# Signalling TensorE's finished groups with a drain in the two edge phases of a four-layer graph network

## The chip, the core and the metric

The kernel runs on one core of one Trainium2 chip. The metric is device time in microseconds (us), the median of several executions. A profile is one further execution, recorded by the hardware profiler. Its span runs from the first to the last recorded instruction.

## What is computed

The reference passes 12,500 node rows of 64 floats through four graph layers, with 200,000 edges sorted by destination. After each layer there is a residual sum and a layer norm. The change lies in the edge work of the last two layers, called Edge 2 and Edge 3 (layers are counted from 0):

```
# layer 2
se = concat([h[src], eh], -1)
msg = leaky_relu(se @ W_msg); q = concat([qrh, qeh], -1) @ W_q / temp; k = se @ W_k
att = sum(q * k, -1); alpha = softmax of att over the edges of one destination
agg = segment_sum(alpha * msg, dst)
# layer 3
combined = concat([node_features[src], edge_features], -1)      # 64 + 32 columns
h_l = relu(combined @ msg_w1[l] + msg_b1[l])                    # two inner layers l
agg = segment_sum(sum over l of (h_l @ msg_w2[l] + msg_b2[l]), dst) / (degree + 1e-8)
```

## The kernel before

The edges lie on 128 partitions, 1,568 on each. An edge phase takes them in chunks of J = 28 edges per partition. That makes 56 chunks, two to each pass of a loop, with buffers b = 0 and 1. Inside a chunk TensorE works in quads of 4 edges per partition, so 7 quads to a chunk, 392 in a phase. Every engine has an instruction stream of its own, written out by hand, and the streams meet only at semaphores. The sequencer of an engine takes its instructions in the order written.

**GpSimd (POOL)** gathers the source rows of a chunk with 28 indirect DMAs (L771). Before them it waits for the chunk's indices and for `rows_free[b]`, which says that the chunk two earlier in this buffer has been read.

**SyncE (SP)** goes chunk by chunk (`EdgePhase.sync`). It waits until the rows are gathered, loads the indices of the chunk two further on (L705), waits for `attr_free[b]`, loads that chunk's attributes (L709), waits for `ready[b]` and stores the finished sums (L712).

**TensorE (PE)** has two functions in each phase. `turn` transposes a quad of gathered and loaded rows into PSUM and then raises `turned`. `multiply` makes the products of a quad that was turned earlier and raises `multiplied`. The order in a chunk is turn 0, turn 1, multiply 0, turn 2, multiply 1, and so on. The last turn of a chunk comes after the sixth multiply instead of before it. After the last turn a drain raises `rows_free[b]`, and in Edge 2 a second drain raises `attr_free[b]`.

**ScalarE (ACT)** copies what was turned from PSUM to SBUF (`move`: L1383 and L1384 in Edge 2, L1592 in Edge 3; it raises `moved`). It also takes the products (`take`: L1391 and L1393 in Edge 2, L1597 in Edge 3; it raises `taken`). It joins the attributes to the rows at a chunk's start (L1400, L1603). After the fourth take of a chunk it lays out the sums of the chunk before (L899), and then `ready` goes up.

**VectorE (DVE)** makes the scores and running softmax (Edge 2) and the running sums (both), and keeps about one chunk behind.

A multiply waits for the quad's `moved` and for an earlier quad's `taken`: the one just before in Edge 2 (`qo_ps` has a single buffer), the one two before in Edge 3. A take waits for its quad's `multiplied`. A move waits for its quad's `turned`. In the profile one float32 matmul of the program is two MATMUL records, a transpose is one. So a turn is 8 records in Edge 2 and 4 in Edge 3, and a multiply is 16 and 8.

Of the kernel before, what the change touches and what calls it, by code (L numbers as in the profile page):

```python
# [31 lines left out]
QUAD = 4  # L32
# [9 lines left out]
def at(i, per, k):  # L42

    return i * per + k
# [1226 lines left out]
def edge_phase_2(p):  # L1271
# [5 lines left out]
    with ExitStack() as ctx:  # L1277
        se = [ctx.enter_context(nc.sbuf_tensor(f"se{b}", [P, J, P], F32)) for b in (0, 1)]
        ph = EdgePhase(p, 2, ctx, p.x_tables[1], lambda b, j: se[b][:, j, 0:FD], quads)
# [4 lines left out]
        q_t = [ph.sb(f"q_t{u}", [P, QUAD, P]) for u in (0, 1)]  # L1284
# [5 lines left out]
        qo_ps = ctx.enter_context(nc.psum_tensor("qo_ps", [P, 2, P], F32))  # L1290
        ps = lambda n: ctx.enter_context(nc.psum_tensor(n, [P, QUAD, P], F32))
        se_ps = [ps(f"se_ps{u}") for u in (0, 1)]
        q_ps = [ps(f"q_ps{u}") for u in (0, 1)]
        mk_ps = [ps(f"mk_ps{u}") for u in (0, 1)]
        joined = ph.sem("joined")
        turned = ph.sem("turned")
        moved = ph.sem("moved")
        multiplied = ph.sem("multiplied")
# [16 lines left out]
        @block.sync  # L1315
        def _(e):
            attr = lambda tiles, name: ([t[:, :, :] for t in tiles], p.ins[name])
            ph.sync(e, [attr(eh, "edge_attr_64"), attr(qr, "edge_attr_64_n2"), attr(qe, "edge_attr_64_n3")])
# [6 lines left out]
        @block.tensor  # L1325
        def _(e):
            e.sem_inc(multiplied, 2)

            def turn(i, b, c):
                n = b * quads + c  # L1330
                u = n % 2
                ph.wait_part(e, i, b, c)
                e.wait_ge(moved, at(i, per, n + 1))
                for j in range(QUAD):
                    e.transpose(se_ps[u][:, j, :], se[b][:, QUAD * c + j, :], p.ident[:, :])
                for s, tile in enumerate((qr, qe)):
                    for half in range(2):
                        j = QUAD * c + 2 * half
                        last = e.transpose(q_ps[u][:, 2 * s + half, :],
                                           tile[b][:, j:j + 2, :].rearrange("p a f -> p (a f)"), p.ident[:, :])  # L1340
                last.then_inc(turned, 1)
                if c == quads - 1:
                    e.drain().then_inc(ph.rows_free[b], 1)  # L1343
                    e.drain().then_inc(ph.attr_free[b], 1)

            def multiply(i, b, c):
                n = b * quads + c
                u = n % 2
                e.wait_ge(moved, at(i, per, n + 3))
                e.wait_ge(taken, at(i, per, n + 2))  # L1350
                e.wait_ge(scored, at(i, per, n + 1))
                for j in range(QUAD):
                    e.matmul(mk_ps[u][:, j, :], se_t[u][:, j, :], p.w2_mk[:, :], start=True, stop=True)  # L1353
                for half in range(2):
                    e.matmul(qo_ps[:, half, :], q_t[u][:, half, :], p.w2_qr[:, :], start=True, stop=False)
                    last = e.matmul(qo_ps[:, half, :], q_t[u][:, 2 + half, :], p.w2_qe[:, :],
                                    start=False, stop=True)
                last.then_inc(multiplied, 1)

            with e.Fori(0, ph.rounds) as i:  # L1360
                for b in (0, 1):
                    ph.wait_attrs(e, i, b, 3)
                    e.wait_ge(joined, at(i, 2, b + 1))
                    turn(i, b, 0)
                    for c in range(quads):
                        if c + 1 < quads - 1:
                            turn(i, b, c + 1)
                        multiply(i, b, c)
                        if c + 1 == quads - 1:
                            turn(i, b, c + 1)  # L1370
            chained.tensor(e)
# [133 lines left out]
def edge_phase_3(p):  # L1505
# [5 lines left out]
    K = 97  # L1511
    with ExitStack() as ctx:
        comb = [ctx.enter_context(nc.sbuf_tensor(f"comb{b}", [P, J, K], F32)) for b in (0, 1)]
        ph = EdgePhase(p, 3, ctx, p.x_tables[2], lambda b, j: comb[b][:, j, 0:FD], quads)
        ea = [ph.sb(f"ea{b}", [P, J, 32]) for b in (0, 1)]
        comb_t = [ph.sb(f"comb_t{u}", [K, QUAD, P]) for u in (0, 1)]
        mask = ph.in_bank(16 * (J + 1)).rearrange("p (f j) -> p f j", f=16)
        ps = lambda n: ctx.enter_context(nc.psum_tensor(n, [P, QUAD, P], F32))
        t_ps = [ps(f"t_ps{u}") for u in (0, 1)]
        h_ps = [ps(f"h_ps{u}") for u in (0, 1)]  # L1520
        joined = ph.sem("joined")
        turned = ph.sem("turned")
        moved = ph.sem("moved")
        multiplied = ph.sem("multiplied")
# [12 lines left out]
        @block.sync  # L1537
        def _(e):
            ph.sync(e, [([t[:, :, :] for t in ea], p.ins["edge_attr_32"])])
# [6 lines left out]
        @block.tensor  # L1546
        def _(e):
            e.sem_inc(multiplied, 2)

            def turn(i, b, c):  # L1550
                n = b * quads + c
                ph.wait_part(e, i, b, c)
                e.wait_ge(moved, at(i, per, n + 1))
                for j in range(QUAD):
                    last = e.transpose(t_ps[n % 2][0:K, j, :], comb[b][:, QUAD * c + j, :], p.ident[:, :])
                last.then_inc(turned, 1)
                if c == quads - 1:
                    e.drain().then_inc(ph.rows_free[b], 1)

            def multiply(i, b, c):  # L1560
                n = b * quads + c
                e.wait_ge(moved, at(i, per, n + 3))
                e.wait_ge(taken, at(i, per, n + 1))
                for j in range(QUAD):
                    last = e.matmul(h_ps[n % 2][:, j, :], comb_t[n % 2][:, j, :], p.w3_hidden[:, :],  # L1565
                                    start=True, stop=True)
                last.then_inc(multiplied, 1)

            with e.Fori(0, ph.rounds) as i:
                for b in (0, 1):  # L1570
                    e.wait_ge(joined, at(i, 2, b + 1))
                    turn(i, b, 0)
                    for c in range(quads):
                        if c + 1 < quads - 1:
                            turn(i, b, c + 1)
                        multiply(i, b, c)
                        if c + 1 == quads - 1:
                            turn(i, b, c + 1)
            chained.tensor(e)
# [978 lines left out]
```

## Time and profile before

| | |
|---|---|
| Median of 3 runs | 12250.41 us (12248.24 to 12255.88) |
| Span of the profiled execution | 12212.0 us, 38.4 us under the median |
| TensorE busy | 2780.2 us, 23% |
| VectorE busy | 4710.0 us, 39% |
| ScalarE busy | 3336.3 us, 27% |
| GpSimd busy | 6789.5 us, 56% |
| Mean granted TensorE clock | 0.579 of full speed |

No run's own time is given for the profiled execution beside its span. The difference of 38.4 us is what lies around the span by the median. Busy shares are averages over all phases. Edge 2 lies between about 5266 and 8710 us of the span, and Edge 3 between about 8960 and 11972 us. In the views, "idle" is the time in which an engine did nothing before an instruction, and "<-" names what ended it. "issue", "remote" and a DMA of another phase stand there when the view found no matching event.

### The profile page before, as it was taken

The page shows a single profiled execution, that of the slowest core. Times are in us where ns is not written, and L with a number is a line of the kernel's source. Part 1 is how long each engine was busy: PE and PEld are TensorE (multiplying, and loading weights), DVE is VectorE, ACT ScalarE, POOL GpSimd, SP SyncE. Part 2 cuts the span into 40 slices and gives each one's busy share as a digit, 9 for nine tenths or more (in the row PEclk, how much of TensorE's full clock was granted, in tenths as well). Part 3 has the DMA queues.
Part 4 walks back from the last instruction along what each step waited for, and adds up shares of the span by engine and source line. Part 5 has one row for each costly group of instructions (what it writes and reads, how often), then busy time and mean ns, then how long its engine had stood idle before and what let it go on. Part 6 is the DMA issues. An engine that isn't in the chain of part 4 may idle for free. (4 is left out here: it accounts for less than half of the span.)

```text
span 12212.0 us, 65741 instructions
## 1 busy us (share of the span) xinstructions
PE 2780.2 (23%) x15715; PEld 2525.3 (21%) x15715; DVE 4710.0 (39%) x6608; ACT 3336.3 (27%) x4637; POOL 6789.5 (56%) x6997
## 2 busy tenths in 40 slices
PE   2000000011000000044444444444333332333333
PEld 1000000010000000034334333333232222322233
DVE  3455555555666666432222222222231111111113
ACT  0222222233222222132222222222242232232231
POOL 6666666657777777644444444444435544544543
PEclk6555555555555555577666667667655555555556
DMA  6232323312222222222222222222111211211121
GB/s 270 91 99 95 98 95 99 99 47 74 98 98 94 98 93 96 69 75 76 76 76 76 76 76 76 75 73 79 39 42 55 63 62 55 63 62 59 59 62 52
DMA packets 366486, 982.75 MB, mean 80 GB/s; under 512 B 163828, under 2 KB 173582, under 8 KB 351652
## 3 DMA queue, kind: packets, MB, share of 16 engines
q1 hardware_dynamic: 135572, 667.06, 14.4%
q0 software_dynamic: 224608, 290.88, 9.4%
q10 hardware_dynamic: 6192, 23.73, 0.5%
q14 instruction: 96, 0.79, 0.0%
q8 instruction: 18, 0.29, 0.0%
HBM read 582.50 MB, written 398.69 MB: 80 GB/s over the span
## 5 line engine op out<-in xcount | busy, mean ns | idle before, releaser
L771 POOL DMA_INDIRECT se<-x_table,edge_ix x1512 | 1428.3, 945 | 1867.2 <-PEq L1343 1397.1
L771 POOL DMA_INDIRECT comb<-x_table,edge_ix x1512 | 1428.8, 945 | 1468.3 <-DMA edge_ix<-in_src 1010.4
L771 POOL DMA_INDIRECT g<-x_table,edge_ix x1512 | 1585.4, 1049 | 512.2 <-issue 512.2
L771 POOL DMA_INDIRECT qv<-qv_table,edge_ix x1484 | 1406.5, 948 | 681.1 <-issue 445.6
L889 DVE TENSOR_TENSOR_SCAN edge_val<-edge_bank,edge_val 128x464 f32<-128x464 f32 (+1 forms) x715 | 687.4, 1031 | 2469.3 <-ACT edge_val L1597 2462.9
L1565 PE MATMUL h_ps<-w_hidden,edge_comb_t 97*128 97x128 f32 x3136 | 699.3, 394 | 1924.3 <-issue 964.5
L899 ACT ACTIVATE edge_sums<-edge_val 128x1904 f32<-128x1904 f32 (+3 forms) x219 | 1107.0, 5055 | 0.0
L1454 DVE TENSOR_TENSOR edge_product<-mk_ps,edge_q_now 128x256 f32<-128x256 f32 x392 | 166.4, 424 | 2364.2 <-ACT edge_msg L1393 2344.8
L1565 PEld LDWEIGHTS h_ps<-w_hidden,edge_comb_t 97*128 97x128 f32 x3136 | 613.2, 291 | 2000.2 <-ACT edge_comb_t L1592 1009.0
L1353 PE MATMUL mk_ps<-w_mk,edge_se_t 128*128 128x128 f32 x3136 | 545.9, 329 | 1659.7 <-issue 1412.0
L1353 PEld LDWEIGHTS mk_ps<-w_mk,edge_se_t 128*128 128x128 f32 x3136 | 483.1, 235 | 1709.1 <-issue 1424.3
L889 DVE TENSOR_TENSOR_SCAN edge_val<-edge_decay,edge_val 128x493 f32<-128x493 f32 (+1 forms) x672 | 714.0, 1131 | 194.5 <-issue 187.6
L842 ACT ACTIVATE edge_bank<-edge_weight_arg 128x112 f32<-128x112 f32 (+3 forms) x169 | 38.6, 228 | 2369.8 <-issue 1557.2
L1597 ACT ACTIVATE edge_val<-h_ps 128x512 f32<-128x512 f32 x392 | 260.8, 665 | 1406.4 <-remote 910.4
L1391 ACT ACTIVATE edge_q_now<-qo_ps 128x256 f32<-128x256 f32 x392 | 151.1, 385 | 1656.4 <-DMA picked<-in_dst_table,found_row_u 1074.0
L1026 PE MATMUL edge_k_ps<-ident,edge_fix_wide 128*128 128x128 f32 x8 | 2.1, 441 | 2315.0 <-DVEq L986 2315.0
L1026 PE MATMUL edge_bond_ps<-ident,edge_fix_wide 128*128 128x128 f32 x4 | 1.2, 461 | 2226.8 <-DVEq L986 2226.8
L1026 PEld LDWEIGHTS edge_k_ps<-ident,edge_fix_wide 128*128 128x128 f32 x8 | 1.8, 327 | 2315.1 <-DVEq L986 2315.1
L1026 PEld LDWEIGHTS edge_bond_ps<-ident,edge_fix_wide 128*128 128x128 f32 x4 | 0.9, 321 | 2226.9 <-DVEq L986 2226.9
L1715 POOL DMA_INDIRECT node_rows<-sums,end_index x392 | 372.9, 951 | 129.4 <-issue 118.2
L1592 ACT ACTIVATE edge_comb_t<-t_ps 97x512 f32<-97x512 f32 x392 | 233.8, 597 | 711.6 <-remote 561.4
L1383 ACT ACTIVATE edge_se_t<-se_ps 128x512 f32<-128x512 f32 x392 | 234.6, 598 | 615.3 <-remote 333.3
(416 smaller groups left out, 9145.2 us busy)
## 6 DMA issues: line engine op xcount, KB each, us to landing
sums<-edge_sums SPq DMA_DIRECT2D x56, 1848.0 KB
sums<-edge_sums SPq DMA_DIRECT2D x55, 1792.0 KB, 6.6
sums<-edge_sums SPq DMA_DIRECT2D x56, 1008.0 KB
sums<-edge_sums SPq DMA_DIRECT2D x55, 924.0 KB, 3.7
edge_k<-k_edges SPq DMA_DIRECT2D x56, 896.0 KB
edge_bond<-in_edge_attr SPq DMA_DIRECT2D x56, 896.0 KB
edge_eh<-in_edge_attr SPq DMA_DIRECT2D x56, 896.0 KB
edge_qr<-in_edge_attr_n SPq DMA_DIRECT2D x56, 896.0 KB
```

What stands on the lines that cost most here:

```text
L771: e.indirect_dma_start(self.gather_into(u, j), None, self.gather_from, bass.IndirectOffsetOnAxis(ap=now[:, j:j + 1], axis=0))\
L842: e.activation(self.weight[:, :, now], self.weight_arg[:, :, now], ACT.Exp).then_inc(self.weighed, 1)
L889: return e.tensor_tensor_scan(out=now, data0=keep[:, 0:n, :].rearrange("p f j -> p (f j)"), data1=now, initial=0.0, op0=ALU.mult, op1=ALU.add)
L899: e.activation(self.sums[b][:, :, 0:n], self.val[b][:, :, 1:].rearrange("p f j -> p j f"), ACT.Copy)\
L1353: e.matmul(mk_ps[u][:, j, :], se_t[u][:, j, :], p.w2_mk[:, :], start=True, stop=True)
L1383: e.activation(se_t[u][:, :, :], se_ps[u][:, :, :], ACT.Copy)
L1391: e.activation(q_now[u][:, :, :], qo_ps[:, :, :].rearrange("p a (c f) -> p (a c) f", c=2), ACT.Copy)
L1454: e.tensor_tensor(product[:, now, :], mk_ps[u][:, :, FD:], q_now[u][:, :, :], ALU.mult)
L1565: last = e.matmul(h_ps[n % 2][:, j, :], comb_t[n % 2][:, j, :], p.w3_hidden[:, :], start=True, stop=True)
L1592: e.activation(comb_t[n % 2][:, :, :], t_ps[n % 2][0:K, :, :], ACT.Copy).then_inc(moved, 1)
L1597: e.activation(into, h_ps[n % 2][:, :, :].rearrange("p j f -> p f j"), ACT.Relu).then_inc(taken, 1)
L1715: e.indirect_dma_start(self.rows[:, t, :], None, self.p.sums[self.layer], bass.IndirectOffsetOnAxis(ap=self.p.end_index[:, t:t + 1], axis=0))\
```

## The change

In `turn` and `multiply` of both phases the last matmul no longer carries the semaphore. A drain of TensorE follows the group and raises it. `rows_free` and `attr_free`, raised by drains of their own before, are raised by plain sequencer increments behind the group's drain.

```
 # Edge 2, turn
-                        last = e.transpose(q_ps[u][:, 2 * s + half, :], ...)
-                last.then_inc(turned, 1)
+                        e.transpose(q_ps[u][:, 2 * s + half, :], ...)
+                e.drain().then_inc(turned, 1)
                 if c == quads - 1:
-                    e.drain().then_inc(ph.rows_free[b], 1)
-                    e.drain().then_inc(ph.attr_free[b], 1)
+                    e.sem_inc(ph.rows_free[b], 1)
+                    e.sem_inc(ph.attr_free[b], 1)
 # Edge 2, multiply
-                    last = e.matmul(qo_ps[:, half, :], q_t[u][:, 2 + half, :], p.w2_qe[:, :], ...)
-                last.then_inc(multiplied, 1)
+                    e.matmul(qo_ps[:, half, :], q_t[u][:, 2 + half, :], p.w2_qe[:, :], ...)
+                e.drain().then_inc(multiplied, 1)
 # Edge 3, turn
-                    last = e.transpose(t_ps[n % 2][0:K, j, :], comb[b][:, QUAD * c + j, :], p.ident[:, :])
-                last.then_inc(turned, 1)
+                    e.transpose(t_ps[n % 2][0:K, j, :], comb[b][:, QUAD * c + j, :], p.ident[:, :])
+                e.drain().then_inc(turned, 1)
                 if c == quads - 1:
-                    e.drain().then_inc(ph.rows_free[b], 1)
+                    e.sem_inc(ph.rows_free[b], 1)
 # Edge 3, multiply
-                    last = e.matmul(h_ps[n % 2][:, j, :], comb_t[n % 2][:, j, :], p.w3_hidden[:, :], ...)
-                last.then_inc(multiplied, 1)
+                    e.matmul(h_ps[n % 2][:, j, :], comb_t[n % 2][:, j, :], p.w3_hidden[:, :], ...)
+                e.drain().then_inc(multiplied, 1)
```

## Rows read from the trace of the kernel before

**Rows 1.** The page's head: the span of the profiled execution.

```profile
span 12212.0 us, 65741 instructions
```

**Rows 2.** Windows of one chunk, Edge 2 and Edge 3: busy, TensorE clock, DMA.

```profile
7011.67:7073.11 61.44, 25.37 (x168) 24.33 (x168) 16.96 (x36) 17.80 (x35) 26.45 (x29) 0.69 0.22 75
10118.72:10172.47 53.75, 16.89 (x84) 15.36 (x84) 9.19 (x11) 16.09 (x18) 26.45 (x28) 0.56 0.20 61
```

**Rows 3.** Waits in Edge 2, 6000 to 8500: total us, times, longest.

```profile
POOL se L771 <- PEq L1343: 1086.4, 41, 26.8
...
ACT edge_q_now L1391 <- DMA picked<-in_dst_table,found_row_u: 814.3, 41, 23.4
```

**Rows 4.** Waits in Edge 3, 9000 to 11900.

```profile
POOL comb L771 <- DMA edge_ix<-in_src: 1010.4, 53, 20.1
...
ACT edge_val L1597 <- remote: 877.8, 104, 21.1
```

**Rows 5.** Timeline of Edge 2, the stall: start, length, instruction, idle before.

```profile
7023.20 0.38 PE L1339 MATMUL q_ps<-ident,edge_qe 128*128 128x128 f32 x2
...
7024.99 0.39 PE L1356 MATMUL qo_ps<-w_qe,edge_q_t 128*128 128x128 f32 x2
...
7025.87 0.38 PE L1339 MATMUL q_ps<-ident,edge_qe 128*128 128x128 f32 x2
...
7031.41 0.60 ACT L1383 ACTIVATE edge_se_t<-se_ps 128x512 f32<-128x512 f32 x1 [8.14 <-issue]
...
7045.40 0.94 POOL L771 DMA_INDIRECT se<-x_table,edge_ix  x1 [0.30 <-issue]
...
7051.03 0.38 ACT L1391 ACTIVATE edge_q_now<-qo_ps 128x256 f32<-128x256 f32 x1 [18.54 <-DMA picked<-in_dst_table,found_row_u]
```

**Rows 6.** Timeline of Edge 2, the quads after the stall.

```profile
7051.79 2.05 PE L1353 MATMUL mk_ps<-w_mk,edge_se_t 128*128 128x128 f32 x8 [25.54 <-issue]
...
7054.91 0.63 PE L1356 MATMUL qo_ps<-w_qe,edge_q_t 128*128 128x128 f32 x2
...
7057.04 1.18 PE L1353 MATMUL mk_ps<-w_mk,edge_se_t 128*128 128x128 f32 x8
...
7058.73 0.39 PE L1356 MATMUL qo_ps<-w_qe,edge_q_t 128*128 128x128 f32 x2
...
7059.61 0.38 PE L1339 MATMUL q_ps<-ident,edge_qe 128*128 128x128 f32 x2
...
7059.91 1.13 PE L1353 MATMUL mk_ps<-w_mk,edge_se_t 128*128 128x128 f32 x8
```

**Rows 7.** Timeline of Edge 2, layout of sums and next gathers.

```profile
7062.63 3.48 ACT L899 ACTIVATE edge_sums<-edge_val 128x1820 f32<-128x1820 f32 x1
...
7073.11 0.95 POOL L771 DMA_INDIRECT se<-x_table,edge_ix  x1 [26.77 <-PEq L1343]
```

**Rows 8.** Timeline of Edge 3, one chunk.

```profile
10127.22 0.60 PE L1555 MATMUL t_ps<-ident,comb 128*97 128x128 f32 x4
...
10130.08 0.60 ACT L1592 ACTIVATE edge_comb_t<-t_ps 97x512 f32<-97x512 f32 x1 [2.20 <-remote]
...
10158.08 0.66 ACT L1597 ACTIVATE edge_val<-h_ps 128x512 f32<-128x512 f32 x1 [12.01 <-remote]
10158.62 6.55 ACT L899 ACTIVATE edge_sums<-edge_val 128x3584 f32<-128x3584 f32 x1
```

**Rows 9.** Timeline at the end of node phase 0.

```profile
2814.19 3.14 PE L1836 MATMUL node_attn_h_ps<-attn_r,node_attn_t 64*128 64x2 f32 x14 [1.05 <-issue]
...
2820.57 0.18 ACT L1960 ACTIVATE node_er<-node_attn_h_ps 128x14 f32<-128x14 f32 x1 [6.43 <-remote]
```

**Rows 10.** The drain at the end of that phase, by source line (columns below).

```profile
L1897 PEldq DRAIN  x1: 7008/7008/7008, 2814.3 to 2814.3; - x1
```

**Rows 11.** Edge 2's two drains by line: count, ns min/median/max, first and last start.

```profile
L1343 PEldq DRAIN  x56: 2180/2930/4073, 5355.2 to 8692.6; - x56
...
L1344 PEldq DRAIN  x56: 13/13/13, 5358.6 to 8694.9; - x56
```

More of the change, by code:

```diff
@@ L1338, in turn @@
                         j = QUAD * c + 2 * half
-                        last = e.transpose(q_ps[u][:, 2 * s + half, :],
-                                           tile[b][:, j:j + 2, :].rearrange("p a f -> p (a f)"), p.ident[:, :])
-                last.then_inc(turned, 1)
+                        e.transpose(q_ps[u][:, 2 * s + half, :],
+                                    tile[b][:, j:j + 2, :].rearrange("p a f -> p (a f)"), p.ident[:, :])
+                e.drain().then_inc(turned, 1)
                 if c == quads - 1:
-                    e.drain().then_inc(ph.rows_free[b], 1)
-                    e.drain().then_inc(ph.attr_free[b], 1)
+                    e.sem_inc(ph.rows_free[b], 1)
+                    e.sem_inc(ph.attr_free[b], 1)
             def multiply(i, b, c):
@@ L1355, in multiply @@
                     e.matmul(qo_ps[:, half, :], q_t[u][:, half, :], p.w2_qr[:, :], start=True, stop=False)
-                    last = e.matmul(qo_ps[:, half, :], q_t[u][:, 2 + half, :], p.w2_qe[:, :],
-                                    start=False, stop=True)
-                last.then_inc(multiplied, 1)
+                    e.matmul(qo_ps[:, half, :], q_t[u][:, 2 + half, :], p.w2_qe[:, :],
+                             start=False, stop=True)
+                e.drain().then_inc(multiplied, 1)
             with e.Fori(0, ph.rounds) as i:
@@ L1564, in multiply @@
                 for j in range(QUAD):
-                    last = e.matmul(h_ps[n % 2][:, j, :], comb_t[n % 2][:, j, :], p.w3_hidden[:, :],
-                                    start=True, stop=True)
-                last.then_inc(multiplied, 1)
+                    e.matmul(h_ps[n % 2][:, j, :], comb_t[n % 2][:, j, :], p.w3_hidden[:, :],
+                             start=True, stop=True)
+                e.drain().then_inc(multiplied, 1)
             with e.Fori(0, ph.rounds) as i:
```

## The prediction, made before the change was run

> **What bounds the kernel now.** I read the page first, for the span of 12212.0 us [rows 1]. The median of the runs is 12250.41, so 38.4 us lie around the span. I make the sum as a difference against the span and add it to the median. Then I read windows of a single chunk. A chunk period is 61.44 us in Edge 2 and 53.75 in Edge 3, and no engine is busy for half of it [rows 2]. So neither phase is bound by an engine's work. Each is bound by a loop of waits.
>
> The waits name the loop. In Edge 2 GpSimd idles 26.5 us a chunk until the drain after the last turn frees the rows (1086.4 over 41), and ScalarE idles 19.9 us a chunk before one take (814.3 over 41) [rows 3]. The view puts that second wait down to a DMA of a phase long over, so its releaser is unknown. The timeline shows what it really is. The last matmul of multiply 0 ends at 7024.99 + 0.39 = 7025.38, nothing else is missing for take 0, and yet take 0 starts at 7051.03. The signal is 25.6 us late. The signal of turn 1 was late too: the transposes end at 7023.58 and the copy starts at 7031.41, 7.8 us later [rows 5]. Multiply 0 and turn 2 ran on meanwhile, up to 7026.25. So the matmuls ran, by their records, and only their semaphores came late.
>
> All this lies inside the gathers. They start at 7011.67 (the window's start) and end at 7045.40 + 0.94 = 7046.34, which is 28 times 1.25 us, and take 0 starts 4.7 us after them [rows 2, 5]. Once they are over, signals are on time again. Edge 3 has the same picture: 2.3 us from the end of a turn (10127.22 + 0.60) to its copy at 10130.08, and takes that idle 877.8 us in total. There the fourth take starts 39.4 us after the chunk's gathers began (10118.72 to 10158.08), the layout of 6.55 us follows, and the next gathers wait for the index load behind it in SP's queue [rows 2, 4, 8].
>
> The loop of Edge 2 is then: gathers start, the late signal of multiply 0 comes 39.4 us later, six more quads run serially between TensorE and ScalarE, the last turn ends, the next gathers start [rows 2, 5, 7].
>
> **The change part by part.** The whole question is whether a drain's semaphore escapes the delay that a matmul's suffers. Edge 2 and 3 have no drain inside the gathers. I found one place in the trace that has one: the end of node phase 0, where indirect DMAs also run. The last matmul ends at 2817.33, and its taker starts only at 2820.57, 3.2 us late [rows 9]. The drain behind it runs 7.008 us from 2814.3, that is to 2821.3. So it ends 0.7 us *after* the late semaphore [rows 9, 10]. In Edge 2, outside the gathers, the drains take 2.93 us by the median, about the length of the group that they wait for, and never above 4.07 [rows 11]. From this one row I take it that the drain waits for the same late completion. The other reading is that the drain was held only because that matmul carried a semaphore, and I keep it as a rival. The Trainium skill, "PSUM — Partial Sum Buffer", section "Engine vs sequencer instructions", says that a drain waits for the engine to go fully idle. By that rule an engine whose completions are late keeps its drain late as well. The row agrees. By the rule the stall of 25.6 us stays, and only costs are added.
>
> *The stall itself: 0.* Turn 1 and multiply 0 still end inside the gathers, and their drains are released at the same 39.4 us.
>
> *The drains on the serial path of Edge 2.* Before, the sequencer queued the next turn behind a multiply while ScalarE took the products, so the turn cost almost nothing. Now the sequencer stands in the drain, and the next group is issued only afterwards. One sequencer step is 0.1 us (the second drain starts 0.1 after the first ends, 5355.2 + 3.27 = 5358.5 to 5358.6 [rows 11]). After a drain come its end, two waits and the first issue, so I take 0.33 us. The bounds are 0.13 (one step) and 0.33. A multiply takes 7055.54 - 7051.79 = 3.75 us at the low clock and 7059.12 - 7057.04 = 2.08 at the high one [rows 6]. A turn has half the records, so I estimate 1.9 and 1.04. Between two multiplies now lie 0.33 + turn + 0.33:
>
> - after multiply 0: 0.33 + 1.9 + 0.33 = 2.56 in place of 7051.79 - 7051.03 = 0.76, so +1.8
> - multiply 1 to 2: 2.56 in place of 7057.04 - 7055.54 = 1.50, so +1.06
> - multiply 2 to 3: 0.33 + 1.04 + 0.33 = 1.70 in place of 7059.91 - 7059.12 = 0.79, so +0.91
> - multiply 3 to 4: hidden by the layout of 3.48 us on ScalarE [rows 7]. Without that cover it would be another 0.9
> - multiply 5 to the last turn's end: 0.33, and 0.17 because the turn's tail no longer overlaps, so +0.5
>
> Together +4.3 us a chunk, times 55 periods = +236. The low bound with 0.13 a drain is 2.9 x 55 = +160. The high bound leaves TensorE at its low level in the later quads too, since it now idles more between groups. Multiplies 2 and 3 then cost 1.7 more each, the gap between them 0.9 more and the last turn 0.9 more: 9.4 x 55 = +517. The granted clock of a chunk is 0.69 in Edge 2, a mix of the two levels, and 0.56 in Edge 3 [rows 2].
>
> *Edge 3.* SP's path needs the fourth take at 39.4 us. Multiply 3 is issued only after turn 4's drain now. Where turn 4 was signalled well before 39.4, nothing changes. Where it is released at the end itself, multiply 3 comes 0.33 + 1.9 = 2.2 us later. I take half the chunks: 1.1 x 55 = +60. Bounds: 0, and 3.8 x 55 = +209 if turn 4 too is issued only behind the end. Later drains of the chunk are covered by the layout of 6.55 us and by the index load; without that cover they would cost 0.9 a quad.
>
> *Drains removed.* `rows_free` and `attr_free` become increments. The second drain took 13 ns [rows 11], and GpSimd waits for the first. Nothing to gain, under 0.1 us a chunk. SP waits for `attr_free` behind its index load, and it moves with the last turn. No DMA is added, and nothing is moved past another queue.
>
> Sum: 12212.0 + 236 + 60 = 12508 in the span, 12250.4 + 296 = **12546 us**. Its own range goes by the bounds from 12250 + 160 + 0 = 12410 to 12250 + 517 + 209 = 12976.
>
> The Trainium skill, "TensorE: Matmul & The Clock Gate", section "Step-by-step: what each phase is for", says that the sequencer takes the next instruction as soon as the engine has the last. Rows 6 show it: the turn ending at 7059.99 hides behind the multiply and the take. The drains end just this, and the rule gives no other sum.
>
> **The rivals.**
>
> *The drain's signal is not late (faster).* The sequencer raises the semaphore, not the matrix array, and only what the array raises may be held back. For it: matmuls go on being executed while their signals wait [rows 5], and the one contrary drain [rows 10] stood behind a matmul that also had a semaphore to deliver. Against it: that drain ended even later than the semaphore. Price: Edge 2 loses 25.6 us of 61.4 and pays 4.3 and about 1 for the first quads, so 41.1 us a chunk, -20.3 x 55 = -1117. Edge 3 becomes bound by its gathers, 28 x 1.25 = 35 us in place of 53.75, -18.7 x 55 = -1030. Time 10100 us. If Edge 3 gains only half, it is about 10600. It decides as soon as a drain shortens the delay of multiply 0 by more than 4.3 us, for then the gain passes the drains' price.
>
> *No difference.* The sequencer steps overlap with ScalarE's copies after all, and what is added falls under the late signals: 12250. Against it, the gaps after 7051 are serial in rows 6, and the first alone adds 1.8 us.
>
> *TensorE stays at the low level.* The slower end of my own case, 12976. For it, the engine idles at each drain. Against it, the clock rises within 5 us of the stall's end today [rows 6].
>
> **How the numbers follow.** The drain is as late as the semaphore and costs the sums above: 0.68, of which 0.12 for the low clock. Signals on time: 0.26. No difference: 0.06. A measurement of this kernel tells about 0.2% (25 us) from no change. So faster 0.26, same 0.06, slower 0.68. The likeliest case's own range is 12410 to 12976. To leave out no more than 2 in 10, the range has to reach across to the fast case: 10050 to 12950.
>
> **What the profile would show.** If I am right, take 0 of Edge 2 still starts 39.4 us after the first gather, drains of 8 to 26 us stand in multiply 0 and turn 1, the multiplies behind lie 0.9 to 1.8 us further apart, and the chunk period is about 65.7 us in Edge 2 and 54 to 56 in Edge 3. If the rival is right, take 0 follows multiply 0 within 0.2 us, GpSimd's idle time falls from 26.8 to some 6 us a chunk in Edge 2 and to near 0 in Edge 3, and VectorE no longer waits. What would make the prediction wrong is one row read too far: the drain of rows 10, whose matmul had a semaphore, where the new drains' matmuls have none.

## The result and the profile after

The changed kernel takes **12589.92 us** (12582.71 to 12594.30, four runs) against 12253.15 for the kernel before (12248.24 to 12259.78, four runs). The ratio is 1.0276, with a 95% interval of 1.0261 to 1.0290. It is slower by 337 us. The forecast was 12546.

The page's head of the kernel after, to be held against [rows 1]:

```profile
span 12591.8 us, 67309 instructions
```

The profiled execution's own time here is 12593.47 us, so only 1.7 us lie around the span. The 38.4 us that the prediction put there were thus no overhead. The profiled execution of before, with a span of 12212.0 us, was a quick one, below all four runs. The two spans differ by 379.8 us, the medians by 336.8. From the first to the last chunk's first gather, Edge 2 grew by 195 us (3336.0 to 3531.0) and Edge 3 by 154 (2932.1 to 3085.9). The other 31 us lie outside these stretches, 11 of them before Edge 2 begins, where both kernels run the same code.

Windows of one chunk, first Edge 2, then Edge 3 (columns as in [rows 2]):

```profile
7057.00:7121.85 64.85, 29.00 (x168) 25.86 (x168) 16.99 (x35) 17.88 (x35) 26.42 (x28) 0.68 0.22 71
9715.81:9772.21 56.40, 22.37 (x84) 18.22 (x84) 9.13 (x10) 16.14 (x17) 26.42 (x29) 0.50 0.20 58
```

ScalarE, VectorE and GpSimd do the same work as in [rows 2]. The chunk is 3.41 us longer in Edge 2 and 2.65 in Edge 3. TensorE is busy for longer, 29.00 us in place of 25.37 and 22.37 in place of 16.89. Edge 3's granted clock fell from 0.56 to 0.50, which is the lower level (1.2 GHz) for the whole chunk. Edge 2's is nearly unchanged (0.69 to 0.68).

Waits in Edge 2, 6000 to 8500, against [rows 3]:

```profile
POOL se L771 <- PEq L1343: 1176.6, 39, 30.3
ACT edge_q_now L1391 <- PEq L1358: 1136.8, 233, 24.2
...
ACT edge_se_t L1383 <- PEq L1341: 485.9, 209, 11.2
```

Waits in Edge 3, 9200 to 12300, against [rows 4]:

```profile
ACT edge_val L1597 <- PEq L1567: 1512.3, 311, 21.1
...
POOL comb L771 <- DMA edge_ix<-in_src: 1160.5, 53, 23.1
```

Two things are to be seen. The view now names a releaser, TensorE's drains (L1341, L1358, L1567), where it had named an old DMA or "remote". And GpSimd waits 1176.6 / 39 = 30.2 us a chunk in place of 26.5 in Edge 2, and 21.9 in place of 19.1 in Edge 3. By the waits that is 3.7 and 2.8 us a chunk, about the whole loss, seen from the engine that starts the next chunk.

The new instructions by source line (count, ns min/median/max, first and last start). The last two rows are the same view of a single chunk, for the turn 1 and the multiply 0 of the window above:

```profile
L1341 PEldq DRAIN  x392: 1040/1070/12033, 5287.8 to 8907.0; - x196
...
L1358 PEldq DRAIN  x392: 1814/1998/39503, 5295.7 to 8909.8; - x196
...
L1567 PEldq DRAIN  x392: 1919/2075/21380, 9186.3 to 12341.4; - x196
...
L1341 PEldq DRAIN  x1: 10803/10803/10803, 7067.5 to 7067.5; - x1
...
L1358 PEldq DRAIN  x1: 17912/17912/17912, 7078.7 to 7078.7; - x1
```

The timeline of that chunk, whose first gather starts at 7057.00:

```profile
7068.80 0.63 PE L1339 MATMUL q_ps<-ident,edge_qe 128*128 128x128 f32 x2
...
7078.35 0.60 ACT L1383 ACTIVATE edge_se_t<-se_ps 128x512 f32<-128x512 f32 x1 [9.95 <-PEq L1341]
...
7081.74 0.44 PE L1356 MATMUL qo_ps<-w_qe,edge_q_t 128*128 128x128 f32 x2
...
7090.71 0.94 POOL L771 DMA_INDIRECT se<-x_table,edge_ix  x1 [0.30 <-issue]
7096.64 0.38 ACT L1391 ACTIVATE edge_q_now<-qo_ps 128x256 f32<-128x256 f32 x1 [17.20 <-PEq L1358]
...
7099.07 2.05 PE L1353 MATMUL mk_ps<-w_mk,edge_se_t 128*128 128x128 f32 x8 [0.32 <-issue]
...
7102.19 0.45 PE L1356 MATMUL qo_ps<-w_qe,edge_q_t 128*128 128x128 f32 x2
...
7104.27 1.13 PE L1353 MATMUL mk_ps<-w_mk,edge_se_t 128*128 128x128 f32 x8 [0.32 <-DVE edge_msg L1455]
...
7105.90 0.39 PE L1356 MATMUL qo_ps<-w_qe,edge_q_t 128*128 128x128 f32 x2
...
7107.91 1.13 PE L1353 MATMUL mk_ps<-w_mk,edge_se_t 128*128 128x128 f32 x8 [0.32 <-DVE edge_msg L1455]
```

The transposes of turn 1 end at 7069.43 by their records, the drain behind them at 7078.3. The last matmul of multiply 0 ends at 7082.18, its drain at 7078.7 + 17.9 = 7096.6, 14.4 us later and 39.6 us after the first gather. Take 0 of before started 39.4 us after the first gather. So the drain is let go where the semaphore was. The Trainium skill, "PSUM — Partial Sum Buffer", section "Engine vs sequencer instructions", says that a drain waits for the engine to go fully idle, and these two drains agree with it. Behind the stall the next multiply starts 7099.07 - 7096.64 = 2.43 us after the take, where it was 0.76 [rows 6].

The timeline of Edge 3 after, in the chunk that begins at 9715.81:

```profile
9736.71 2.04 PE L1565 MATMUL h_ps<-w_hidden,edge_comb_t 97*128 97x128 f32 x8 [4.61 <-issue]
9753.98 0.67 ACT L1597 ACTIVATE edge_val<-h_ps 128x512 f32<-128x512 f32 x1 [16.93 <-PEq L1567]
...
9754.15 1.14 PE L1555 MATMUL t_ps<-ident,comb 128*97 128x128 f32 x4 [15.39 <-issue]
...
9755.68 2.04 PE L1565 MATMUL h_ps<-w_hidden,edge_comb_t 97*128 97x128 f32 x8 [0.40 <-issue]
9757.78 0.67 ACT L1597 ACTIVATE edge_val<-h_ps 128x512 f32<-128x512 f32 x1 [1.77 <-PEq L1567]
9758.33 6.57 ACT L899 ACTIVATE edge_sums<-edge_val 128x3584 f32<-128x3584 f32 x1
```

And one row of the kernel before, multiply 3 of the chunk in [rows 8]:

```profile
10146.12 2.08 PE L1565 MATMUL h_ps<-w_hidden,edge_comb_t 97*128 97x128 f32 x8 [13.79 <-issue]
```

Before, multiply 3 was already executed inside the stall (10146.12), and the end of the stall released its take. After, take 2 starts at 9753.98, that is 38.17 us into the chunk, and only then are turn 4 and multiply 3 issued, one after the other, each behind a drain. The fourth take starts at 41.97 us in place of 39.36.

Not every chunk looks so. In the one that begins at 9659.62 take 2 comes earlier, at 34.6 us, and turn 4 is issued at once, but its own signal is held:

```profile
9694.42 1.14 PE L1555 MATMUL t_ps<-ident,comb 128*97 128x128 f32 x4 [15.42 <-issue]
9699.16 0.60 ACT L1592 ACTIVATE edge_comb_t<-t_ps 97x512 f32<-97x512 f32 x1 [4.25 <-PEq L1556]
...
9701.53 0.66 ACT L1597 ACTIVATE edge_val<-h_ps 128x512 f32<-128x512 f32 x1 [1.77 <-PEq L1567]
```

The transposes end at 9695.56 by their records, the copy starts 3.6 us later, and the fourth take starts at 41.9 us all the same.

### The profile page after: what moved, and what is told of

It is laid out like the page before. It is cut to its first block and busy times, and to the rows that moved or that the text cites. A ratio compares the mean times of both kernels' runs of the same rounds, so it can differ in the third digit from the quotient of the medians.

```text
span 12591.8 us, 67309 instructions
## 1 busy us (share of the span) xinstructions
PE 3267.0 (26%) x15715; PEld 2753.3 (22%) x15715; DVE 4716.1 (37%) x6608; ACT 3344.9 (27%) x4637; POOL 6782.5 (54%) x6997
## 5 line engine op out<-in xcount | busy, mean ns | idle before, releaser
L1565 PE MATMUL h_ps<-w_hidden,edge_comb_t 97*128 97x128 f32 x3136 | 805.0, 438 | 654.5 <-issue 385.5
L1565 PEld LDWEIGHTS h_ps<-w_hidden,edge_comb_t 97*128 97x128 f32 x3136 | 697.8, 327 | 778.4 <-issue 474.2
L1555 PE MATMUL t_ps<-ident,comb 128*97 128x128 f32 x1568 | 449.1, 440 | 1274.7 <-issue 1157.0
L1353 PE MATMUL mk_ps<-w_mk,edge_se_t 128*128 128x128 f32 x3136 | 594.9, 349 | 693.4 <-issue 437.7
L1353 PEld LDWEIGHTS mk_ps<-w_mk,edge_se_t 128*128 128x128 f32 x3136 | 513.0, 248 | 791.9 <-issue 568.6
L1335 PE MATMUL se_ps<-ident,se 128*128 128x128 f32 x1568 | 326.0, 345 | 1327.2 <-issue 1284.5
L842 ACT ACTIVATE edge_bank<-edge_weight_arg 128x112 f32<-128x112 f32 (+3 forms) x169 | 38.6, 228 | 2371.3 <-issue 1423.9
L1555 PEld LDWEIGHTS t_ps<-ident,comb 128*97 128x97 f32 x1568 | 323.3, 273 | 1383.8 <-issue 1329.1
L1335 PEld LDWEIGHTS se_ps<-ident,se 128*128 128x128 f32 x1568 | 214.7, 174 | 1408.8 <-issue 1396.5
```

The costliest lines, as they stand in the source:

```text
L842: e.activation(self.weight[:, :, now], self.weight_arg[:, :, now], ACT.Exp).then_inc(self.weighed, 1)
```

## The experiments

Each time is a median beside the kernel before on the same chip. The last two columns are us from one chunk's first gather to the next's, by the median of all chunks in the trace.

| kernel | time us | before us | ratio (95%) | Edge 2 | Edge 3 |
|---|---|---|---|---|---|
| before | | 12253.15 | | 61.44 | 53.76 |
| after | 12589.92 | 12253.15 | 1.0276 (1.0261 to 1.0290) | 64.85 | 56.40 |
| edge2_only | 12435.92 | 12246.68 | 1.0151 (1.0134 to 1.0168) | 64.85 | 53.94 |
| turns_only | 12347.79 | 12246.68 | 1.0086 (1.0069 to 1.0103) | 61.44 | 55.49 |
| mults_only | 12303.74 | 12246.68 | 1.0046 (1.0029 to 1.0063) | 61.60 | 54.07 |
| drains_added | 12574.29 | 12246.68 | 1.0264 (1.0246 to 1.0281) | 64.84 | 56.31 |
| thin_before | 9203.56 | 12259.27 | 0.7509 (0.7497 to 0.7522) | 34.07 | 26.74 |
| thin_after | 9689.92 | 12259.27 | 0.7905 (0.7892 to 0.7918) | 37.51 | 32.04 |
| pause_short | 11650.13 | 12259.27 | 0.9504 (0.9488 to 0.9520) | 52.78 | 51.97 |
| pause_long | 14914.75 | 12259.27 | 1.2171 (1.2151 to 1.2191) | 81.78 | 80.90 |
| bare_drain4 | 11267.64 | 12250.65 | 0.9196 (0.9181 to 0.9212) | 50.35 | 47.37 |
| fill7 | 10663.16 | 12250.65 | 0.8703 (0.8688 to 0.8718) | 44.30 | 42.28 |
| short_after | 11678.95 | 12250.65 | 0.9532 (0.9516 to 0.9548) | 52.85 | 52.38 |
| bare_drain7 | 9927.67 | 8991.09 | 1.1042 (1.1027 to 1.1057) | 44.89 | 41.68 |

**Is it the drain's signal, or the drain's presence?** In `drains_added` the semaphores stay on the last matmul, as before, and a bare drain follows each group.

```
                 last.then_inc(multiplied, 1)
+                e.drain()
```

> The kernel before with a bare drain behind every turn and multiply, and all semaphores left on the last matmuls. My theory: a drain waits for the same late completion whether or not the matmul has a semaphore, and the whole price is that TensorE's sequencer stands in it: as the changed kernel, 12590 to 12610. Rival, that a drain behind matmuls without a semaphore ends earlier: then this one is slower than the changed kernel by that, by up to several us in each of 110 chunks, 12700 or more. Second rival, that moving the semaphore itself costs: then this one is close to 12253.

It takes 12574.29 us, +328 against its own before, where the change took +337. The chunk periods are those of the changed kernel to 0.1 us. So moving the semaphore to the drain costs nothing that shows in the time. The sequencer standing in the drain, and not issuing the next group, is the price. Within an Edge 2 chunk the two kernels do differ. By the medians the take of multiply 5 starts 62.32 us after the first gather (62.69 in the changed kernel), and the next gathers start 2.52 us after that take (2.16), behind one drain more. The two differences nearly cancel. Its drains by source line (L1342 behind turns, L1360 behind multiplies of Edge 2):

```profile
L1342 PEldq DRAIN  x392: 1090/1488/12602, 5282.9 to 8900.2; - x196
...
L1360 PEldq DRAIN  x392: 1853/2025/38253, 5290.9 to 8903.0; - x196
```

**How the price is shared by the phases.** `edge2_only` takes Edge 3 back to the kernel before.

```
 # Edge 3, turn and multiply
-                e.drain().then_inc(turned, 1)
+                last.then_inc(turned, 1)
```

> The change in Edge 2 alone, Edge 3 as before. My theory: the cost is what the drains add to the serial path between TensorE and ScalarE, separately in each phase. The chunk period of Edge 2 went from 61.44 to 64.85 us in the changed kernel, so 3.4 x 55 = 188 us: 12440. Rival, that Edge 3 carries the whole cost: 12253. A sum of the two parts that differs from the 337 us of the whole by more than 30 would mean that the phases are not independent.

+189 us, of 337 in all. Edge 3 is back at its old period. 3.41 us by 55 periods is 188. That is as expected. Edge 3's share is the rest, about 148, and 2.65 by 55 is 146.

**Which of the two drains costs it.** `turns_only` leaves the drains behind the turns and puts the multiplies' semaphore back on the last matmul, `mults_only` the other way round.

```
 # turns_only, both phases
-                e.drain().then_inc(multiplied, 1)
+                last.then_inc(multiplied, 1)
```

> Drains signal the turns alone, the multiplies keep the last matmul's semaphore, in both phases. My theory: a turn is still queued behind the running multiply, only the next multiply has to wait for the drain and about 0.3 us of sequencer steps. That is about 1.3 us behind the stall, 0.6 at the low clock and 0.4 at the high one, some 2.3 us a chunk in Edge 2 and near 0 in Edge 3: 12380. Rival, that every drain costs the same wherever it stands: half of the 337 us, 12420, and as much in the other half.

> Drains signal the multiplies alone, the turns keep the last transpose's semaphore. My theory: this is the dearer half, because the turn behind a multiply is issued only after it, while ScalarE's copies used to cover it: about 3 us a chunk in Edge 2 and 1 to 2 in Edge 3, 12460 to 12500. Take 0 still starts about 39.4 us after the first gather. Rival (equal price): 12420.

`mults_only` was a plain miss: +57 us, where I had expected it to be the dear one. `turns_only` cost +101. From the first to the last chunk's first gather it is 90 us longer than before in Edge 3 and 23 in Edge 2, `mults_only` 28 and 42. Neither moves the median period of Edge 2 by more than 0.2 us, and together they cost 3.4. What differs is multiply 5, the sixth of a chunk's seven. This is its first eight records in the timelines of before, of `turns_only` and of `mults_only`:

```profile
7068.02 2.05 PE L1353 MATMUL mk_ps<-w_mk,edge_se_t 128*128 128x128 f32 x8 [3.27 <-ACT edge_q_t L1384]
```

```profile
7389.12 1.13 PE L1353 MATMUL mk_ps<-w_mk,edge_se_t 128*128 128x128 f32 x8 [2.84 <-ACT edge_q_t L1384]
```

```profile
7031.56 1.13 PE L1353 MATMUL mk_ps<-w_mk,edge_se_t 128*128 128x128 f32 x8 [3.02 <-ACT edge_msg L1393]
```

Before, TensorE is at its lower level for this multiply, behind 3.27 us of idle time (2.05 us). With one kind of drain the clock is still at its higher level there (1.13 us). Over all chunks, these eight records take more than 1.6 us in 52 of 56 before, in 3 of `turns_only` and in 12 of `mults_only`. By the medians, the take of multiply 5 comes 1.4 us sooner after the one before it in `turns_only` and 1.3 in `mults_only`. This gift of the clock hides what the drains cost elsewhere in the chunk. In the changed kernel the multiply runs at the lower level again (2.05 us from 7116.02, over 1.6 us in 53 of 56 chunks) and the gift is gone, though the idle time before it is shorter there, 2.44 us. It does not go by the number of drains: `drains_added` has both kinds, and there the median is 1.38 us, with 5 of 56 over 1.6. What decides the level was not tried and stays open.

**Does the stall come from the gathers, and is it part of the price?** The `thin` pair gathers only 7 of a chunk's 28 columns in Edge 2 and 3. The other source rows stay zero, so the output is not the reference's.

```
-                    if J * n + j < done:
+                    if J * n + j < done or (self.k >= 2 and j % QUAD >= 1):
                         continue
```

> The kernel before, but Edge 2 and 3 gather only one column in four (7 indirect DMAs a chunk in place of 28, the other columns hold zeros), so the output is not the reference's. My theory: late completions belong to the stretch from some 6 us after the first gather to 4.7 us after the last one. With gathers of 8.75 us that ends at 13.4 us. Take 0 of Edge 2 then comes at about 14 us in place of 39.3, the chunk period falls by 25 us to about 36, and Edge 3 falls from 53.8 to about 29: 9500 to 9700 us. Rival, that the late signals come from something else (attribute loads, TensorE itself) and only happen to fall into the gathers: take 0 stays where it is in relation to turn 1, periods stay within 5 us of 61.4 and 53.8, 11700 to 12250.

> The changed kernel with the same thinning (7 gathers a chunk, output not the reference's). It shows the drains' price where hardly a signal is late. My theory: every gap between groups is now on the path, so the price is higher than the 337 us of the full kernel: about 4 to 6 us a chunk in Edge 2 and 1 to 4 in Edge 3, in all 300 to 500 over the thinned kernel before. Rival, that the drain's signal is quicker than the matmul's as soon as the backlog is short: this one is the faster of the two.

Windows of one chunk of `thin_before`, Edge 2 and Edge 3:

```profile
5786.72:5820.78 34.06, 23.68 (x168) 22.41 (x168) 17.00 (x35) 17.92 (x35) 6.62 (x7) 0.85 0.30 116
8476.25:8502.98 26.73, 15.73 (x84) 14.41 (x84) 9.04 (x10) 15.53 (x17) 6.61 (x7) 0.63 0.27 93
```

The same of `thin_after`:

```profile
5690.50:5728.01 37.51, 24.87 (x168) 21.81 (x168) 17.01 (x35) 17.93 (x35) 6.60 (x7) 0.86 0.28 105
8643.59:8675.64 32.05, 22.39 (x84) 18.24 (x84) 9.14 (x10) 16.12 (x17) 6.61 (x8) 0.50 0.23 81
```

With a quarter of the gathers, the take of multiply 0 starts 14.3 us into the chunk in place of 39.3, as expected, and the total falls further than expected (9203.56, against 9500 to 9700). The drains then cost 486 us in place of 337: 3.4 us a chunk in Edge 2 as before, but 5.3 in Edge 3 in place of 2.65. In this kernel the signal of multiply 0 isn't late. By the medians that multiply ends 14.3 us into the chunk, 5.8 us behind the last of the seven gathers (4.2 in the chunk shown), so it no longer falls among them:

```profile
5800.58 0.39 PE L1361 MATMUL qo_ps<-w_qe,edge_q_t 128*128 128x128 f32 x2
...
5801.00 0.39 ACT L1396 ACTIVATE edge_q_now<-qo_ps 128x256 f32<-128x256 f32 x1 [1.11 <-PE qo_ps L1361]
```

So the stall does not make the drains dear. In Edge 3 it covers half of their price, because the first quads wait for the stall's end anyway. A part of the 5.3 us is the clock: the window's granted clock is 0.50 in place of 0.63, and how much of it that is was not separated. Nor does the pair tell whether GpSimd's issuing or the transfers themselves hold the signals, since thinning takes away both.

**Does a pause of GpSimd let the signals through?** Here the kernel before gets gaps inside the gathers: `pause_short` a fill of 128x512 and a drain of GpSimd behind every fourth gather, `pause_long` eight of them.

```
+                    if self.k >= 2 and j % 4 == 3:
+                        for _ in range(1):        # 8 in pause_long
+                            e.memset(self.idle[:, :], 0.0)
+                            e.drain()
```

> The kernel before, with a short GpSimd fill of 128x512 and a drain behind every fourth gather in Edge 2 and 3 (some 0.5 to 0.8 us, output unchanged). If gaps between gathers let completions through (gathers come every 1.25 us with 0.3 between), some late signals come earlier: take 0 of Edge 2 at one of the first gaps, 15 to 25 us, and the kernel is faster by several per cent, 11000 to 12000. If only the end of the whole burst releases them: the burst grows by 7 x 0.6 = 4 us a chunk and the kernel is slower by 110 x 4 = 440 us, 12700.

> As pause_short with eight such fills behind every fourth gather, some 4 to 5 us, as long as the 4.7 us that the last gather's signals need. My theory: by then every completion is through, so each pause releases all that is late, and take 0 comes about 15 us after the first gather. The burst grows to 35 + 7 x 4.5 = 66 us and becomes the bound itself if TensorE's work fits beside it: periods of 66 to 70 in both phases, 13000 us. If pauses of this length do not release either: 61.4 + 31 a chunk, 15500.

`pause_short` is 5% faster than the kernel before. Its gaps are 2.3 to 2.4 us long, but in Edge 2 the first of each chunk is 5.8 us, for a reason that was not looked for. By the medians the takes in Edge 2 now start 3.5, 21.7, 28.1, 35.3, 42.3, 49.4 and 52.2 us after a chunk's first gather, where before none started between 2.5 and 39.3. No take or copy of the two phases starts more than 1.5 us after both its TensorE group and ScalarE's instruction before it are over. So the takes no longer wait for late signals, and it is GpSimd that sets the pace: 28 gathers and seven gaps fill the period. In `pause_long` no signal is late either. Its gaps alone, some 6.9 us each, longer than I had reckoned, make 80.9 us a chunk.

**Is it the fill or the drain, and how many gaps are needed?** `bare_drain4` has GpSimd's drain alone, `fill7` a fill and a drain behind every seventh gather.

```
 # bare_drain4
+                    if self.k >= 2 and j % 4 == 3 and j < J - 1:
+                        e.drain()
 # fill7
+                    if self.k >= 2 and j % 7 == 6 and j < J - 1:
+                        e.memset(self.idle[:, :], 0.0)
+                        e.drain()
```

> The kernel before with a bare GpSimd drain behind every fourth gather of Edge 2 and 3 except the last (output unchanged). The fill and drain of the 11650 us kernel opened gaps of 2.3 to 2.5 us, and each released one round of signals. If the gap's being there is what counts and a drain alone opens 1 to 1.7 us, the burst is 35 + 6 x 1.4 = 43 us and the period 45 to 50: 11000 to 11500. If the gap must be at least 2 us, signals stay late, and the burst's growth makes it 61 to 70 a chunk: 12300 to 12800.

> The fill and drain of pause_short behind every seventh gather instead of every fourth, three gaps a chunk in place of seven. One round of signals (one quad) is let through at each gap. My theory: three gaps let three quads through in a burst of 35 + 3 x 2.2 = 42 us, the other quads follow at 2.8 to 3.6 us each: period about 42 + 4.7 + 3 x 3.5 = 57 in Edge 2, 52 in Edge 3: 12000. If gaps release all that follows for some time, period 45: 10700.

The bare drain opens gaps of some 2.3 us too (the second of an Edge 2 chunk is 5.4) and does nearly the same. With three gaps in place of seven the kernel is faster still, 10663 us, which was the rival's number: seven quads do not need a gap each. The timeline of `fill7` in Edge 2 (L773 is the gather, L1361 the multiply's last line, L1396 the take):

```profile
6795.58 0.95 POOL L773 DMA_INDIRECT se<-x_table,edge_ix  x1 [0.30 <-issue]
...
6796.28 0.39 PE L1361 MATMUL qo_ps<-w_qe,edge_q_t 128*128 128x128 f32 x2
...
6798.08 0.94 POOL L773 DMA_INDIRECT se<-x_table,edge_ix  x1 [0.30 <-issue]
6799.02 0.54 POOL L777 MEMSET edge_idle<- 128x512 f32 x1
6800.63 0.38 ACT L1396 ACTIVATE edge_q_now<-qo_ps 128x256 f32<-128x256 f32 x1 [3.25 <-DMA picked<-in_dst_table,found_row_u]
...
6801.41 0.95 POOL L773 DMA_INDIRECT se<-x_table,edge_ix  x1 [1.85 <-issue]
```

The matmul ends at 6796.67, 6.1 us into a run of gathers that began at 6790.57. Its signal comes at 6800.63, in the gap, 4.0 us late. In this chunk signals in the first 4 to 5 us of a run are on time, later ones wait for its end.

**The drains beside the pauses.** `short_after` is the changed kernel with the pauses of `pause_short`.

> The changed kernel with the fill and drain of pause_short on GpSimd. It asks whether the drain's signal is better where completions are let through now and then. My theory: a turn and a multiply now each need a gap of their own, since the second is issued only when the first is through, so one quad takes up to two gaps: period 60 to 70 in place of 52.8, 12300 to 13000. Rival, that the drains cost only their 0.33 us a group: period 55 to 56, 11900 to 12000.

It takes 0.9532 of before, and `pause_short` 0.9504. Both expectations were too high. The chunk is 52.85 and 52.38 us against 52.78 and 51.97. With the gaps, GpSimd's own run of 28 gathers and its pauses sets the period, and TensorE's drains lie under it, but for 0.1 us in Edge 2 and 0.4 in Edge 3.

**The same with bare drains, and another chip.** `bare_drain7` has GpSimd's drain alone behind every seventh gather.

```
+                    if self.k >= 2 and j % 7 == 6 and j < J - 1:
+                        e.drain()
```

> A bare GpSimd drain behind every seventh gather except the last (three a chunk, output unchanged), as fill7 without the fill. In bare_drain4 the bare drain opened the same gap of 2.3 us as fill and drain did. My theory: the drain alone clears the backlog and the fill does nothing: 10550 to 10680, against 10663 with the fill. Rival, that the fill's work on GpSimd matters: signals are late again behind the gaps, 11000 or more.

It fell on another chip, and there **the kernel before takes 8991.09 us** (8985.98 to 8994.98, nine runs) in place of the 12247 to 12259 of the three chips of the other experiments. The gaps make the kernel slower there, 1.1042. Its timeline in Edge 2, inside a run of gathers that began at 6888.33 (L1358 is the multiply, L1393 the take, L1341 the turn, L1385 the copy):

```profile
6895.22 0.39 PE L1358 MATMUL qo_ps<-w_qe,edge_q_t 128*128 128x128 f32 x2
6895.64 0.38 ACT L1393 ACTIVATE edge_q_now<-qo_ps 128x256 f32<-128x256 f32 x1 [1.74 <-PE qo_ps L1358]
...
6895.81 0.94 POOL L771 DMA_INDIRECT se<-x_table,edge_ix  x1 [0.30 <-issue]
...
6896.48 0.38 PE L1341 MATMUL q_ps<-ident,edge_qe 128*128 128x128 f32 x2
...
6896.90 0.60 ACT L1385 ACTIVATE edge_se_t<-se_ps 128x512 f32<-128x512 f32 x1 [0.60 <-PE q_ps L1341]
```

The signals come 0.03 and 0.04 us after the modelled ends, seven and eight us into the run. In `fill7` the multiply that ended 6.1 us into its run had a signal 4.0 us late. Over both phases of `bare_drain7` none of 1,560 takes and copies starts more than 0.2 us after both its TensorE group and ScalarE's instruction before it are over. Both kernels have runs of 14 gathers in Edge 3. Of the groups that end more than 10 us into such a run, 106 of 110 in `fill7` have a signal over 0.5 us late, and none of 143 in `bare_drain7`. The gather itself is spaced the same, 1.25 us. Edge 0's gathers, which no experiment touches, are a little faster. This is their group of lines in the kernel before on the first chip, and in `bare_drain7`:

```profile
L771 POOL DMA_INDIRECT g<-x_table,edge_ix x1512 | 1585.4, 1049 | 512.2 <-issue 512.2
```

```profile
L771 POOL DMA_INDIRECT g<-x_table,edge_ix x1512 | 1426.7, 944 | 460.8 <-issue 460.8
```

So the late signals belong to the chip, or its state, as much as to the kernel. The two kernels also differ by `fill7`'s fills, but the kernel before, which has none, takes a quarter less time on this chip. There is no trace of it there. The times of `bare_drain7` and `fill7` can't be compared, and no run shows what the drains of this change cost on such a chip.

## Why the prediction was right, and where its terms were off

**The stall: right.** Take 0 of Edge 2 starts 39.59 us after the first gather by the median (39.32 before). The drains of turn 1 and multiply 0 last 10.8 and 17.9 us in the chunk shown, and 9.8 and 18.6 by the medians, within the 8 to 26 foretold. The one row from node phase 0 [rows 10] carried over to matmuls without a semaphore.

**Edge 2: right in kind, +3.4 in place of +4.3 a chunk.** By the medians of the takes, the terms came out so:

| term | predicted | measured |
|---|---|---|
| take 0 | 0 | +0.27 |
| after multiply 0 | +1.8 | +1.54 |
| multiply 1 to 2 | +1.06 | +0.03 |
| multiply 2 to 3 | +0.91 | +0.83 |
| multiply 3 to 4 (layout) | 0 | 0.00 |
| multiply 4 to 5 | 0 | +0.22 |
| multiply 5 to the next gathers | +0.5 | +0.52 |

One term failed, multiply 1 to 2. I gave the turn there 1.9 us, the lower level's length. Its drain took 1.07, the length of the higher level, so that the gap became 7104.27 - 7102.64 = 1.63 us where it had been 1.50. The clock had risen one group sooner than I took it to. The sequencer's steps fit. Where nothing else is waited for, a drain that ends is followed by the next drain 0.23 to 0.40 us later, against my 0.33.

**Edge 3: right in kind, the size was off.** +2.65 a chunk in place of +1.1. The whole of it arises at the fourth take (41.95 us in place of 39.38 by the medians). The layout and the index load follow at their old distances, as foretold. The failed step is "I take half the chunks". In each of the 54 chunks in the middle of the phase the fourth take starts 2.40 to 2.44 us after turn 4's drain ends, and that drain ends at 39.5 us by the median (38.7 to 40.9), where the fourth take itself started before. So the case "released at the end itself", priced at 2.2 us, holds in every chunk and not in half. It has two forms. In 19 chunks turn 4 is issued at 32.7 to 37.6 us and its drain is held. In the other 35 it is issued only at 38.3 to 39.8 us, the form that I had kept as a bound of 3.8, and the price is no higher because take 2 comes at 38.1 to 39.5 us there. So 146 us stand where I had 60.

**The total was nearer than its terms.** The two errors have opposite signs, 236 + 60 = 296 foretold against 188 + 146 = 334, and the total fell 44 us from the mark. Part of that nearness is luck.

**The rivals.** That the drain's signal is not late is refuted by the drains of 10.8 and 17.9 us, and `drains_added` shows that the semaphore's place has no part in the price that the time would show. No difference is refuted by the interval. TensorE staying at the lower level came true in Edge 3 (0.50) and not in Edge 2, where multiplies 2 and 3 still run at 1.13 us for their first eight records. In Edge 3 the distances between the takes from the fourth to the sixth stay as they were, so most of its cost lies under the stall and the layout.

**One sentence of mine is less sure than it stood there:** "the matmuls ran, by their records, and only their semaphores came late". The Trainium skill, "Perfetto Trace Analysis", section "Tensor Engine Instruction (MATMUL, LD_WEIGHTS)", says that a matmul's end in the profile is estimated, and that the semaphore is pushed only when PSUM has acknowledged the writes. No run here shows that acknowledgement. By the rule on drains above, TensorE did not count as idle for its own sequencer until the signal came. Whether the array, the write or its acknowledgement was held stays open.

## What to carry to other kernels

A drain behind a group costs the overlap of that group with the next: here 3.4 and 2.6 us a chunk of seven quads, though a second drain with nothing to wait for took 13 ns [rows 11]. A completion that was late for the semaphore was late for the drain too, so moving the signal from one to the other did not outrun it. Where a view names an old DMA or "remote" as the releaser, compare the end of the work with the start of its taker, and look at what else ran between: the larger gain here, 13% with `fill7`, lay in the gathers and not in TensorE's signals, and it has to be measured on more than one chip.

## What the runs showed of the hardware that was not expected

- While GpSimd issued indirect DMAs without a gap, completions of TensorE came late on three chips. In Edge 2 of the kernel before, turn 1 was 7.8 us late, still among the gathers, and multiply 0 25.6 us, 4.7 us after the last of 28. Among the same gathers none of 58 starts of VectorE behind ScalarE's takes, and none of 55 of ScalarE behind VectorE (L842), was over 0.04 us late.
- A drain on GpSimd behind a gather opened a gap of about 2.3 us (up to 5.9 at one place of an Edge 2 chunk), and late signals came in it. Three gaps a chunk, with a fill in each, took the kernel from 12250.65 to 10663.16 us.
- On one other chip no signal was late in `bare_drain7`, the kernel before took 8991.09 us, and the gaps only cost (9927.67). What differs between the chips was not found.
- In Edge 2 the level of TensorE's clock in multiply 5, 1.13 or 2.05 us for eight records, changed with small shifts of work elsewhere in the chunk. It was worth 1.4 us a chunk, as much as a kind of drain.
